# Routing of the first batch inside the state-space layer's last sequence, batches of 6, 5 and 5, and a third gather buffer

## The chip, the cores and the metric

The kernel runs on one core of a Trainium2 chip. The metric is the device time of one execution in microseconds (us); lower is better. Before the change the median of three runs is 1745.33 us (1744.99 to 1748.70).

The core's engines run side by side, each with its own instruction stream: PE multiplies matrices (weights are loaded by PEld), DVE does vector work, ACT applies functions, POOL does vector work too and issues the indirect DMAs (gathers and scatters), and SP issues the plain DMAs. They wait for each other by semaphores.

## The reference

The input is 16 sequences of 512 rows of 128 numbers. Four blocks follow each other, each with a residual and a layer norm:

```python
x = layernorm(x + linear_attention(x, W))                  # block 1
x = layernorm(x + moe32(x))                                # block 2: 32 experts, top 4, plus a shared expert
x = layernorm(x + mamba(x))                                # block 3: selective state space, 16 states
x = layernorm(x + moe8(x))                                 # block 4: 8 experts, top 2, plus a shared expert

def moe8(x):                       # xf: 8192 rows
    scores = softmax(xf @ gate_w.T)
    _, idx = top_k(scores + gate_b, 2)                     # the choice is by the biased scores,
    w = take_along_axis(scores, idx)                       # the weight by the unbiased ones
    expert(x) = silu((x @ w1 + b1) * (x @ w3 + b3)) @ w2 + b2
    return sum_k w[k] * expert[idx[k]](x) + shared_expert(x)

def mamba(x):                      # per sequence, d_inner 256
    xi, z = split(x @ in_proj.T); xc = silu(conv(xi))
    h_t = exp(dt_t * A) * h_(t-1) + dt_t * x_t * B_t       # 16 states, 512 steps
    y_t = sum_n h_t[n] * C_t[n] + D * x_t
    return (y * silu(z)) @ out_proj.T
```

## The kernel before

**Blocks 1 and 2** (0 to 376 us). The rows are normalized and stored with their gates in `xg_rows`. The 32 experts are worked through in eight groups of four. For a group, POOL gathers the rows (`xe<-xg_rows`, L759, four indirect DMAs), PE transposes and multiplies (L1255 to L1271), ACT and DVE form the gated product, DVE writes `ye` (L1651), and POOL adds the result into `resid_rows` (L767, four indirect DMAs). There are two `xe` buffers: the first two groups are gathered up front, and while group s is scattered, one scatter and one gather in turn, group s + 2 is gathered.

**Block 3** (376 to 1371 us). The 16 sequences run through a software pipeline, `schedule(iteration)`: in the turn of a sequence s, DVE scans its 16 states n one after the other (two scans `hst` of 512 steps, L1757, and for 12 of the 16 states the product `prod` with C, L1779; POOL makes the other four, L834); ACT makes the decays (L1029), POOL `dbx` (L825), PE sums over the states (L1340). In the same turn the front of the next sequence f (projections, convolution) and the end of the one before, m (`y` L1692, out-projection L1353, statistics L1511, scale and shift on POOL from L809, `x3o` on ACT), are spread over the states. In the last sequence's turn there is no f. Its place is used for the first batch of block 4: PE transposes its kept rows (L1363), ACT copies them (L1060), and PE scores them (L1372), one sequence at each of the states 7 to 12.

**Block 4** (1371 to 1741 us). The rows are cut into batches of 6, 6 and 4 sequences (`BATCH`). Of each batch DVE works out the routing: `scores` (row maximum and difference, L1705 and L1707), ACT the exponential (`soften`, L1070), `choose` and `choose_second` (L1713 to L1743, the two best of eight experts), PE counts (L1464), `place_rows` (L1847 to L1865) and `place_rows_end` (L1873 to L1892: the row numbers `row_of`, the gates and the table of units). Then POOL scatters the batch's rows, sorted by expert, into `sorted_rows` (`send_rows`, L880, two indirect DMAs a tile of 128 rows). PE runs 60 steps g: `N_FIRST` = 12 shared steps (one sequence each through the shared expert), then 44 routed units of 512 sorted rows (16, 16 and 12 in the three batches), then the other four shared steps (`LATE`). A step is L1421 (transpose), L1430, L1433, L1446 and L1456/L1457 on PE. The units' results are stored in `expert_rows`; POOL fetches them back (`fetch_rows`, L892, eight indirect DMAs a sequence) and DVE adds them up (`combine`) at the steps of `COMBINE_AT`. Rows of a batch can be fetched when all units of the batch are stored.

All orders are written out by hand: each engine's program lists its instructions in the order of the states and steps.

## Time and profile before

| | |
|---|---|
| median of three runs | 1745.33 us |
| profiled execution, its own time | 1742.75 us |
| its span | 1741.0 us |
| mean granted PE clock | 0.896 |
| PE busy | 1393.9 us, 80% |
| DVE busy | 1352.9 us, 78% |
| POOL busy | 1367.5 us, 79% |
| ACT busy | 972.2 us, 56% |
| POOL dbx L825, 256 of them | 613.8 us |
| DVE scans L1757, 512 of them | 592.0 us |
| POOL fetches L892, 128 of them | 124.5 us, 50.7 idle before them |
| POOL scatters L880, 128 of them | 125.9 us, 48.4 idle before them |

The profile is of one execution; its times stand beside its own 1742.75, which is 2.6 us below the median. The busy shares are means over four blocks that are limited by different engines: a share of 80% says nothing of what a stretch waits for. For that one reads a stretch at a time. An entry in square brackets names how long the engine was idle before an instruction and what ended the wait. "issue" is time in which the profile shows nothing that the engine waited for.

### The profile page before, as it was taken

The numbers are of one execution on the slowest core, as the hardware profiler recorded it, in microseconds if no ns is written. First come the engines' busy times: TensorE is split into PE (matmuls) and PEld (weight loads), VectorE is DVE, ScalarE is ACT, GpSimd is POOL, SyncE is SP. The second block draws the span as 40 slices with busy tenths as digits, with TensorE's granted clock in tenths as the row PEclk, the third lists the DMA queues.
The fourth block names the chain that finished last, engine by engine and source line by source line (L and its number), as shares of the span: only waits on it lengthen the run. The fifth ranks groups of instructions, "written<-read, shape, count | busy, mean of one in ns | idle before, by whom it ended". The sixth has DMA issues, their size and how long they took to land.

```text
span 1741.0 us, 23137 instructions
## 1 busy us (share of the span) xinstructions
PE 1393.9 (80%) x5849; PEld 832.6 (48%) x5890; DVE 1352.9 (78%) x2623; ACT 972.2 (56%) x1681; POOL 1367.5 (79%) x949
## 2 busy tenths in 40 slices
PE   5778744426998899889988998898897797999990
PEld 3666643312443344334433443343343476998970
DVE  3888831112999999999999999999999858657777
ACT  2665511104655665566556646655664465887873
POOL 2656566753999999999989989999999477777575
PEclk8999955557999999999989999999899999999995
DMA  5433243325382422342234123312521323555544
GB/s 149 127 101 121 84 89 59 43 40 187 117 254 115 141 84 73 123 140 73 80 127 140 62 86 132 133 56 90 178 80 55 118 69 97 165 155 155 147 107 135
DMA packets 195131, 195.44 MB, mean 112 GB/s; under 512 B 22520, under 2 KB 174008, under 8 KB 190776
## 3 DMA queue, kind: packets, MB, share of 16 engines
q1 hardware_dynamic: 172280, 168.95, 30.0%
q0 software_dynamic: 22784, 25.71, 7.3%
q8 instruction: 28, 0.46, 0.1%
q14 instruction: 39, 0.32, 0.1%
HBM read 137.26 MB, written 59.80 MB: 113 GB/s over the span
## 4 chain that ended last, share of the span: by engine, by line
PE 42%; DVE 26%; issue 15%; POOL 9%; ACT 2%; DMA 2%; DVEq 1%; SPq 1%; POOLq 0%; another core or an unknown queue 0%; ACTq 0%
PE bank L1340 13%; DVE hst L1757 12%; PE bank L1295 6%; PE bank L1433 2%; DVE prod L1779 2%; PE bank L1446 2%; POOL dbx L825 2%; PE bank L1430 2%; PE bank L1457 2%; PE bank L1456 2%; POOL yg L892 2%; PE bank L1329 1%; PE bank L1353 1%; PE bank L1293 1%; POOL xe L759 1%
## 5 line engine op out<-in xcount | busy, mean ns | idle before, releaser
L825 POOL TENSOR_TENSOR dbx<-u,ball 128x1024 f32<-128x1024 f32 x256 | 613.8, 2497 | 5.3 <-POOL u L862 2.8
L1757 DVE TENSOR_TENSOR_SCAN hst<-bank,dbx 128x512 f32<-128x512 f32 x512 | 592.0, 1205 | 11.2 <-POOL dbx L825 6.7
L1340 PE MATMUL bank<-prod,ident 128*128 128x512 f32 x1024 | 514.0, 639 | 23.4 <-DVE prod L1779 18.0
L1029 ACT ACTIVATE bank<-dt,aneg 128x511 f32<-128x511 f32 x512 | 346.4, 688 | 278.8 <-DVE hst L1757 276.8
L1340 PEld LDWEIGHTS bank<-prod,ident 128*128 128x128 f32 x1024 | 207.4, 205 | 263.6 <-issue 209.9
L1779 DVE TENSOR_TENSOR prod<-hst,bank 128x1024 f32<-128x1024 f32 x192 | 233.4, 1216 | 17.2 <-DVE hst L1757 13.8
L834 POOL TENSOR_TENSOR prod<-hst,call 128x1024 f32<-128x1024 f32 x64 | 161.0, 2515 | 22.9 <-DVE hst L1757 22.8
L892 POOL DMA_INDIRECT yg<-expert_rows,row_of x128 | 124.5, 972 | 50.7 <-issue 38.5
L1324 PE MATMUL bank<-parts,sel_c 128*128 128x512 bf16 x152 | 61.1, 403 | 73.8 <-DVE prod L1779 73.1
L1295 PE MATMUL bank<-x2T,inc 128*128 128x512 f32 x256 | 116.5, 598 | 0.0
L880 POOL DMA_INDIRECT sorted_rows<-x3b,row_of x80 | 79.3, 991 | 27.9 <-issue 25.3
L1324 PEld LDWEIGHTS bank<-parts,sel_c 128*128 128x128 bf16 x192 | 18.8, 98 | 132.5 <-DVE prod L1779 88.3
L1802 DVE SCALAR_TENSOR_TENSOR hg<-bank,wv,ha 128x256 f32<-128x256 f32 x88 | 38.5, 479 | 55.4 <-ACT ha L1083 55.1
L1295 PEld LDWEIGHTS bank<-x2T,inc 128*128 128x128 f32 x256 | 49.3, 193 | 62.7 <-issue 62.7
L694 POOL TENSOR_TENSOR dga<-rka,iota_a 128x2048 bf16<-128x2048 f32 x16 | 58.7, 3670 | 12.3 <-DVE ohb L1540 12.3
L1456 PE MATMUL bank<-wv,hg 128*128 128x128 f32 x352 | 68.1, 275 | 0.4 <-DVE acc L1833 0.4
L1457 PE MATMUL bank<-wv,hgb 128*128 128x128 f32 x352 | 68.2, 276 | 0.0
L767 POOL DMA_INDIRECT resid_rows<-ye,ixs x32 | 50.7, 1585 | 16.2 <-issue 13.7
L880 POOL DMA_INDIRECT sorted_rows<-x3a,row_of x48 | 46.6, 970 | 20.5 <-issue 13.4
L857 POOL TENSOR_TENSOR dt<-dtr,dta 128x1024 f32<-128x1024 f32 x16 | 40.7, 2545 | 27.3 <-ACT dta L1022 27.3
L1456 PEld LDWEIGHTS bank<-wv,hg 128*128 128x128 f32 x352 | 56.8, 192 | 3.2 <-DVE acc L1833 0.6
L710 POOL TENSOR_SCALAR rstd<-mv 128x4 f32<-128x4 f32 x16 | 3.6, 228 | 67.8 <-DVE mv L1584 67.8
(294 smaller groups left out, 2765.4 us busy)
## 6 DMA issues: line engine op xcount, KB each, us to landing
ball<-b_rows SPq DMA_DIRECT2D x32, 2048.0 KB, 7.1
call<-b_rows SPq DMA_DIRECT2D x16, 1024.0 KB, 9.5
xr<-sorted_rows SPq DMA_DIRECT2D x44, 256.0 KB
expert_rows<-yu SPq DMA_DIRECT2D x44, 256.0 KB, 2.7
sorted_rows<-blank SPq DMA_DIRECT2D x2, 4096.0 KB
xg_rows<-xg SPq DMA_DIRECT2D x16, 320.0 KB, 2.5
xt<-in_x SPq DMA_DIRECT2D x16, 256.0 KB, 2.9
xT<-in_xT SPq DMA_DIRECT2D x16, 256.0 KB, 3.1
```

Source lines behind the costliest of these rows:

```text
L825: gp.tensor_tensor(dbx[n % NDB][:, :, :], u[s.par][:, :, :], ball[:, n:n + 1, :].to_broadcast([P, NH, SEQ]), ALU.mult).then_inc(dbx_rdy, 1)
L834: gp.tensor_tensor(prod[2][:, :, :], hst[2][:, :, :], call[:, k:k + 1, :].to_broadcast([P, NH, SEQ]), ALU.mult).then_inc(pprod_rdy, 1)
L880: gp.indirect_dma_start(xs_d[b][:, :], bass.IndirectOffsetOnAxis(row_of[:, c, k:k + 1], 0), x3_tile(k), None).then_inc(sent[k % 2], 16)
L892: gp.indirect_dma_start(yg[q % 3][:, k, c, :], None, y_d[b][:, :], bass.IndirectOffsetOnAxis(row_of[:, c, q * TT + k:q * TT + k + 1], 0)). ...
L1029: act.activation(da_ps[h][:, 1:SEQ], dt_[s.par][:, h, 1:SEQ], ACT.Exp, scale=aneg[:, h, n:n + 1]).then_inc(da_rdy, 1)
L1295: last = mm(pb_ps[:, :], inc[:, k, tile(h)], x2T[:, k:k + SEQ], start=False, stop=(k == DCONV - 1))
L1324: mm(cb_ps[k % 2][:, :], sel_c[:, n, :], parts[s.par][:, :], start=True, stop=True).then_inc(cb_rdy, 1)
L1340: last = mm(y_ps[:, h, :], ident[:, :], from_[:, h, :], start=False, stop=(n == NS - 1), skip_group_check=True)
L1456: mm(yu_ps[g % 2][:, tile(k)], hg[g % 2][:, tile(k)], w[:, W2A:W2B], start=True, stop=False)
L1457: last = mm(yu_ps[g % 2][:, tile(k)], hgb[g % 2][:, tile(k)], w[:, W2B:BIAS], start=False, stop=True)
L1757: dve.tensor_tensor_scan(h_of[:, h, :], da_ps[h][:, :], dbx[n % NDB][:, h, :], 0.0, ALU.mult, ALU.add).then_inc(scan_rdy, 1)
L1779: tt(prod[k % 2][:, :, :], h_of[:, :, :], over_h(cb_ps[k % 2]), ALU.mult).then_inc(prod_rdy, 1)
```

## The change

1. **Third `xe` buffer.** `NXE = 3`: POOL gathers three groups up front, and group s + 3 while group s is scattered. The loops over groups on PE, DVE and POOL are written out. One wait on `xe_got` is added before the indices of the next gather.
2. **Routing of the first batch** moves on DVE from behind the last sequence into its turn: `scores` behind state 9's product, `choose` and `choose_second` in state 10, `place_rows` and `place_rows_end` behind state 11's product. The gates and the table of units are split off (`gates_and_units`) and stay behind y. ACT copies the kept rows at the states 3, 4, 6 (two), 7 (two), in place of one at each of 7 to 12, and its exponential `soften` stands in state 10.
3. **Scatters of the first batch**: five tiles (ten DMAs) on POOL at state 15, four tiles (eight) before the last scale and shift, the other thirty where all 48 stood.
4. **Batches of 6, 5, 5**, units 16, 14, 14. The shared step of sequence 1 goes from the first ones behind the units (`LATE` has five), and `COMBINE_AT` moves with it.

```diff
-BATCH = (6, 6, 4)
+BATCH = (6, 5, 5)
+NXE = 3
-LATE = (2, 3, 4, 5)
-S_ORDER = (0,) + tuple(range(6, NB)) + (1,) + LATE
+LATE = (1, 2, 3, 4, 5)
+S_ORDER = (0,) + tuple(range(6, NB)) + LATE
+KEPT_TURN = {3: ((0, None),), 4: ((1, None),), 6: ((2, 0), (3, 1)), 7: ((4, 2), (5, 3)), 8: ((None, 4), (None, 5))}
+SCORE_0, CHOOSE_0, COUNT_0, PLACE_0 = 9, 10, 11, 11
+SENT_FIRST, SENT_NEXT = 5, 4
-COMBINE_AT = [35, 37, 39, 41, 43, 45, 49, 51, 53, 56, 58, 60, 61, LAST, LAST, LAST]
+COMBINE_AT = [34, 36, 39, 41, 43, 45, 48, 50, 52, 55, 57, 61, 62, LAST, LAST, LAST]
-            xe = [eb(f"xe{p}", [P, EG, XGW]) for p in range(2)]
+            xe = [eb(f"xe{p}", [P, EG, XGW]) for p in range(NXE)]
...
# POOL, a group of experts
                 if ahead:
+                    gp.wait_ge(xe_got[ahead.par], ahead.half(16 * EG))
                     take_indices(ixg, ahead, ixg_rdy)
...
-            with gp.bass.Fori(0, E0 // EG // 2 - 1, engines=(gp.engine,), hint_back_edge=True) as j:
-                for i in (0, 1):
-                    group(Seq(j, i), Seq(j, i + 2))
-            group(Seq(0, E0 // EG - 2), None)
-            group(Seq(0, E0 // EG - 1), None)
+            for i in range(E0 // EG):
+                group(Seq(0, i), Seq(0, i + NXE) if i + NXE < E0 // EG else None)
...
# POOL, the state-space layer
             def iteration(f, s, m, ahead):
                 for n in range(NS):
+                    if s and not f and n == NS - 1:
+                        gp.wait_ge(ld_x3[0], X3_LOADS[0])
+                        send_rows(0, range(SENT_FIRST))
...
+                    if m and not s and n == 3:
+                        send_rows(0, range(SENT_FIRST, SENT_FIRST + SENT_NEXT))
                     if m and n == 4:
                         scale_shift(rs2, nm2, mv2, m, m_mv, m_rs, x3_rdy)
...
# DVE, the state-space layer
-                    if m and not s and n == 0:
-                        dve.wait_ge(pprod_rdy, NP * NB)
-                        scores(0)
                     if m and n == 0:
                         gated(m)
-                    if m and not s and n == 1:
-                        choose(0)
-                        choose_second(0)
+                    if m and not s and n == 0:
+                        gates_and_units(0)
...
+                    if s and not f and n == SCORE_0:
+                        dve.wait_ge(dt_rdy, NB)
+                        dve.wait_ge(u_rdy, NB)
+                        scores(0)
+                    if s and not f and n == CHOOSE_0:
+                        choose(0)
+                        choose_second(0)
+                    if s and not f and n == PLACE_0:
+                        place_rows(0)
+                        place_rows_end(0)
```

The batch's PE count goes to state 11, the two banks of `l1_ps` change places, and the tiles of block 4 in SBUF are laid out in another order.

DVE, from the last states of the last sequence on, before (`hst` are the scans of states, `l1m`, `l1s` the scores, `y2` the gated output, `l1z` the first instruction of `choose`):

```order
L1757 SCALAR_TENSOR_TENSOR hst1<-bank2,dbx3 128x512
L1757 SCALAR_TENSOR_TENSOR hst1<-bank3,dbx3 128x512
L1779 TENSOR_TENSOR prod1<-hst1,bank56 128x1024
L1705 TENSOR_REDUCE l1m<-lg0 128x24
L1707 TENSOR_TENSOR l1s<-lg0,l1m 128x192
L1692 TENSOR_TENSOR y2<-zs1,bank01 128x1024
L1713 TENSOR_REDUCE l1z<-l1e 128x24
L1715 RECIPROCAL l1r<-l1z 128x24
L1717 TENSOR_TENSOR sc1<-l1e,l1r 128x192
```

and now, at states 9 to 10 of the same sequence (lines have other numbers: L1833 is the scan, L1851 the product, L1719 and L1721 the scores, L1727 on `choose`):

```order
L1851 TENSOR_TENSOR prod0<-hst0,bank4 128x1024
L1719 TENSOR_REDUCE l1m<-lg0 128x24
L1721 TENSOR_TENSOR l1s<-lg0,l1m 128x192
L1833 SCALAR_TENSOR_TENSOR hst2<-bank2,dbx2 128x512
L1833 SCALAR_TENSOR_TENSOR hst2<-bank3,dbx2 128x512
L1727 TENSOR_REDUCE l1z<-l1e 128x24
L1729 RECIPROCAL l1r<-l1z 128x24
L1731 TENSOR_TENSOR sc1<-l1e,l1r 128x192
L1733 TENSOR_TENSOR bi1<-sc1,w_gb1 128x192
```

Scores and choice have moved from behind the last product to between the scans, with six more scan pairs behind them.

POOL, behind the last `dbx` of the last sequence, before (`hgb` are the memsets, `rs2` and `nm2` scale and shift):

```order
L825 TENSOR_TENSOR dbx3<-u1,ball 128x1024
L842 MEMSET hgb0 64x512
L843 MEMSET hgb0 64x512
L842 MEMSET hgb1 64x512
L843 MEMSET hgb1 64x512
L809 TENSOR_SCALAR rs2<-mv2 128x4
L811 TENSOR_TENSOR rs2<-rs2,neghalf 128x4
L814 TENSOR_TENSOR nm2<-mv2,rs2 128x4
L817 TENSOR_SCALAR nm2<-nm2 128x4
L880 DMA sorted_rows0<-x3a,row_of 8192x128 x48
```

and now (L849 is the send):

```order
L831 TENSOR_TENSOR dbx3<-u1,ball 128x1024
L849 DMA sorted_rows0<-x3a,row_of 8192x128 x10
L860 MEMSET hgb0 64x512
L861 MEMSET hgb0 64x512
L860 MEMSET hgb1 64x512
L861 MEMSET hgb1 64x512
L849 DMA sorted_rows0<-x3a,row_of 8192x128 x8
L815 TENSOR_SCALAR rs2<-mv2 128x4
L817 TENSOR_TENSOR rs2<-rs2,neghalf 128x4
L820 TENSOR_TENSOR nm2<-mv2,rs2 128x4
L823 TENSOR_SCALAR nm2<-nm2 128x4
L849 DMA sorted_rows0<-x3a,row_of 8192x128 x30
```

Ten sends now stand before the memsets and eight between these and the scale and shift.

ACT, in the last sequence, now (L1074 copies kept rows, L1041 makes decays):

```order
L1041 ACTIVATE bank2<-dt1,aneg 128x511
L1041 ACTIVATE bank3<-dt1,aneg 128x511
L1074 ACTIVATE xu0<-bank56 128x512
L1074 ACTIVATE xu1<-bank56 128x512
L1041 ACTIVATE bank2<-dt1,aneg 128x511
L1041 ACTIVATE bank3<-dt1,aneg 128x511
L1074 ACTIVATE xu0<-bank56 128x512
L1074 ACTIVATE xu1<-bank56 128x512
```

Before, each of the six copies stood alone between two pairs of decays; now four of them stand two by two.

## Rows read from the trace of the kernel before

**Rows 1.** the stretches view: us of the stretch, busy us and count by engine, granted clock
```profile
1311.00:1369.00 58.00, 48.20 (x172) 25.32 (x175) 54.84 (x58) 25.44 (x42) 45.92 (x27) 0.97 0.02 7
1396.90:1419.70 22.80, 22.80 (x139) 17.06 (x137) 8.82 (x13) 12.92 (x21) 17.27 (x19) 1.00 0.16 53
1484.60:1532.70 48.10, 48.10 (x323) 45.03 (x321) 28.47 (x61) 40.03 (x81) 35.59 (x36) 1.00 0.57 162
```

**Rows 2.** timeline of POOL, first expert layer: start, us, instruction, [idle before <-releaser]
```profile
270.81 0.18 POOL L756 COPY ixs<-idx 128x4 uint32 x1 [7.01 <-DVE ye L1651]
...
339.96 0.20 POOL L756 COPY ixs<-idx 128x4 uint32 x1
...
353.77 0.20 POOL L756 COPY ixs<-idx 128x4 uint32<-128x4 uint32 x1
...
366.05 0.19 POOL L756 COPY ixs<-idx 128x4 uint32<-128x4 uint32 x1 [3.45 <-DVE ye L1651]
```

**Rows 3.** timeline of DVE: y of three sequences, then the last sequence's end
```profile
487.20 1.22 DVE L1692 TENSOR_TENSOR y<-zs,bank 128x1024 f32<-128x1024 f32 x1 [0.35 <-PE bank L1340]
...
778.93 1.22 DVE L1692 TENSOR_TENSOR y<-zs,bank 128x1024 f32<-128x1024 f32 x1
...
1256.77 1.22 DVE L1692 TENSOR_TENSOR y<-zs,bank 128x1024 f32<-128x1024 f32 x1 [1.63 <-PE bank L1340]
...
1348.13 2.34 DVE L1757 TENSOR_TENSOR_SCAN hst<-bank,dbx 128x512 f32<-128x512 f32 x2 [1.11 <-ACT bank L1029]
...
1365.66 0.34 DVE L1705 TENSOR_REDUCE l1m<-lg 128x24 f32<-128x192 f32 x1
...
1367.82 1.22 DVE L1692 TENSOR_TENSOR y<-zs,bank 128x1024 f32<-128x1024 f32 x1 [1.42 <-PE bank L1340]
...
1375.40 0.83 DVE L1511 BATCH_NORM_STATS2 st<-bank 128x6 f32<-128x128 f32 x4
...
1376.68 0.33 DVE L1847 COPY tin<-bank 128x192 f32<-128x192 f32 x1
...
1381.62 0.19 DVE L1880 CAST row_of<-posf 128x48 uint32<-128x48 f32 x1
```

**Rows 4.** the chain of waits, last batch's fetches: start, us, what
```profile
1687.65 0.35 POOL yg L892
...
1726.52 0.94 POOL yg L892
```

**Rows 5.** timeline of DVE, end of the first expert layer
```profile
365.18 0.69 DVE L1651 TENSOR_TENSOR ye<-bank,ge 128x512 f32<-128x512 f32 x1 [4.20 <-PE bank L1271]
376.39 0.23 DVE L1783 TENSOR_SCALAR negb<-ident 128x128 bf16<-128x128 f32 x1 [10.52 <-DMA resid_rows<-ye,ixs]
```

**Rows 6.** timeline of ACT, last sequence: a copy of kept rows
```profile
1346.82 0.60 ACT L1060 ACTIVATE xu<-bank 128x512 f32<-128x512 f32 x1 [2.58 <-PE bank L1363]
```

**Rows 7.** timeline of PE: out-projection, first new sequence, first unit
```profile
1369.09 2.05 PE L1353 MATMUL bank<-w_outp,y 128*128 128x128 f32 x16 [0.46 <-DVE y L1692]
...
1380.13 1.09 PE L1421 MATMUL bank<-ident,x3b 128*128 128x128 f32 x4 [3.95 <-DMA x3b<-x_rows]
...
1450.50 0.63 PE L1421 MATMUL bank<-ident,xr 128*128 128x128 f32 x4 [0.25 <-DMA xr<-sorted_rows]
1454.85 0.89 PE L1421 MATMUL bank<-ident,xr 128*128 128x128 f32 x4 [3.72 <-ACT xu L1065]
```

**Rows 8.** timeline of POOL behind the last scan
```profile
1364.55 0.52 POOL L842 MEMSET hgb<- 64x512 f32 x1 [7.09 <-DVE hst L1757]
...
1376.95 0.23 POOL L809 TENSOR_SCALAR rs<-mv 128x4 f32<-128x4 f32 x1 [10.20 <-DVE mv L1515]
```

**Rows 9.** the page's groups: POOL's long product
```profile
L825 POOL TENSOR_TENSOR dbx<-u,ball 128x1024 f32<-128x1024 f32 x256 | 613.8, 2497 | 5.3 <-POOL u L862 2.8
```

**Rows 10.** one line each: durations ns min/median/max, first and last start
```profile
L1579 DVE TENSOR_TENSOR gm<-lexp,mask x16: 272/273/336, 41.2 to 227.1; 128x128 f32<-128x128 f32 x16
...
L811 POOL TENSOR_TENSOR rs<-rs,neghalf x32: 1036/1040/1165, 386.7 to 1377.3; 128x4 f32<-128x4 f32 x32
```

More of the change, by code:

```diff
@@ L367, in build @@
         tab = sb("tab", [P, 2 * N_UNIT], I32)
+        ha = [sb(f"ha{k}", [P, SEQ]) for k in range(2)]
+        hab = [sb(f"hab{k}", [P, SEQ]) for k in range(2)]
+        hg = [sb(f"hg{k}", [P, SEQ]) for k in range(2)]
+        hgb = [sb(f"hgb{k}", [P, SEQ]) for k in range(2)]
+        yu = [sb(f"yu{k}", [P, TT, D]) for k in range(3)]
+        yg = [sb(f"yg{k}", [P, TT, 2, D]) for k in range(3)]
+        st3 = sb("st3", [P, TT, 6])
+        mv3 = sb("mv3", [P, NB * TT, 2])
+        rs3 = sb("rs3", [P, NB * TT])
+        nm3 = sb("nm3", [P, NB * TT])
         wall = sb("wall", [P, E1, WCOLS])
@@ L783, in group @@
                         gather(ahead, k)
-            for i in (0, 1):
+            for i in range(NXE):
+                need(gp, xe_got[i % 2], 16 * EG * (i // 2))
                 take_indices(ixg, Seq(0, i), ixg_rdy)
@@ L1039, in iteration @@
                         front(f, n)
-                    if s and not f and 7 <= n < 7 + KEPT:
-                        kept_up(n - 7)
-                    if s and not f and n == 7 + KEPT:
+                    if s and not f and n in KEPT_TURN:
+                        for k, scored in KEPT_TURN[n]:
+                            if k is not None:
+                                kept_up(k)
+                    if s and not f and n == SCORE_0 - 1:
                         act.wait_ge(l1_mm, KEPT)
@@ L1254, in group @@
                 for k in range(EG):
-                    last = pe.transpose(bank[2][:, tile(k)], xe[s.par][:, k, 0:D], ident[:, :])
+                    last = pe.transpose(bank[2][:, tile(k)], xe[s.off % NXE][:, k, 0:D], ident[:, :])
                 last.then_inc(xeT_mm, 1)
@@ L1272, in group @@
                 last.then_inc(dn_mm, 1)
-            with pe.bass.Fori(0, E0 // EG // 2, engines=(pe.engine,), hint_back_edge=True) as j:
-                for i in (0, 1):
-                    group(Seq(j, i))
+            for i in range(E0 // EG):
+                group(Seq(0, i))
             def front(s, n):
@@ L1396, in iteration @@
                         out_proj(m)
-                    if s and not f and 7 < n <= 7 + KEPT:
-                        kept_score(n - 8)
-                    if s and not f and 7 <= n < 7 + KEPT:
-                        kept_turn(n - 7)
+                    if s and not f and n in KEPT_TURN:
+                        for k, scored in KEPT_TURN[n]:
+                            if scored is not None:
+                                kept_score(scored)
+                            if k is not None:
+                                kept_turn(k)
+                    if s and not f and n == COUNT_0:
+                        count(0)
             pe.wait_ge(added, E0 // 2 * 16)
@@ L1664, in _ @@
             group(Seq(0, 1))
-            with dve.bass.Fori(1, E0 // EG // 2, engines=(dve.engine,), hint_back_edge=True) as j:
-                for i in (0, 1):
-                    group(Seq(j, i))
+            for i in range(2, E0 // EG):
+                group(Seq(0, i))
             def stats_ahead(s):
```

171 lines of the change are left out of this document (82 added, 89 removed).

## The prediction, made before the changed kernel was run

> **What bounds the kernel now.** I read the page's busy shares first: no engine is at its limit over the whole span, so the stages have to be read one by one. [rows 1] gives three stretches. In the last sequence of the state-space layer (1311 to 1369) DVE is busy 54.84 of 58.00 us and PE 48.20. In four shared steps of the last layer (from 1396.9) PE is busy throughout at full clock, 22.80 us for four, 5.70 each, and DVE needs 8.82, 2.2 a step. In ten routed units (from 1484.6) PE is again full, 48.10 us, 4.81 each, and DVE has 28.47, 2.8 a unit. Then the timelines, engine by engine, where the edit moves work. In the first expert layer POOL's indirect DMAs set the pace [rows 2]. In the last sequence DVE's chain of scans does [rows 3]. At the very end POOL does once more: fetch after fetch, the chain of waits being nothing but POOL L892 and its issue gaps [rows 4].
>
> **A. Third gather buffer, first expert layer: -8.4 us.** In [rows 2] a group of four scatters with four gathers takes 339.96 to 353.77, 13.8 us; one with scatters alone runs from 353.77 to 362.60 (366.05 less the 3.45 of idle time before it), 8.8 us. The four gathers are the difference, 5.0, 1.25 each. Before, two groups are without gathers; now three are, and the four gathers taken away stand up front, before the first scatter. Up front POOL idles 7.01 us before 270.81, waiting for DVE's first ye: the four gathers (5.0) and a copy of indices fit. So one group gets shorter by 13.8 - 8.8 = 5.0. The second gain: POOL waits 3.45 us before 366.05 for DVE's ye at 365.18 [rows 5]; the last group's rows now arrive a whole group earlier, so ye is done when POOL comes. Sum 5.0 + 3.4 = 8.4. The layer's end hangs on the last scatter: DVE waits 10.52 us for resid_rows at 376.39 [rows 5]. The new wait on `xe_got` names gathers issued a group ago: nothing. Loops written out cost or save nothing that a row shows. Bounds: 0 (something else sets the group's pace) and -9 (issue gaps go too).
>
> **B. Routing of batch 0 inside the last sequence: +16.5 us.** A state costs DVE 3.5 us there: from 1348.13 to 1365.66 are five of them, 17.5 us, with one wait, of 1.11 [rows 3]. So nothing that is put in is hidden. What is put in, with its durations from where it stood: scores two instructions behind 1365.66, 0.34 us the first, 0.74 together; choose, first and second best, from y's end at 1369.0 to the statistics at 1375.40, 6.4; place 1376.68 to 1381.81, 5.1; together 12.2 [rows 3]. On top come waits. The copies of kept rows come two to a turn now, and ACT's exponentials stand behind them: ACT waited 2.58 us for PE before a single such copy [rows 6], and DVE's scans take what the exponentials make; l1e is asked for one state after the scores, with an exponential pair in front of it on ACT; the count on PE answers after two small matmuls. I take 1 + 1 + 1 us for pairs of copies, 0.8 for the rest, and 0.5 for issue between small instructions: 12.2 + 3.8 + 0.5 = 16.5.
> What it takes away behind the sequence is less than it seems. Before, choose stood between y (1367.82) and the statistics (1375.40) and held these back 4.3 us, the end of PE's out-projection being 1371.1 [rows 7]. But PE's first shared step on a new sequence waits for the DMA x3b until 1380.13, 3.95 us [rows 7], and that load is issued when the out-projection is done, whatever DVE does. x3o, which PE's last matmul group of the first shared step waits for, is held from the other side: POOL's scale_shift began at 1376.95, 12.4 us after the last scan (1364.55) [rows 8]. Now four memsets (2.2) and eight sends stand before it on POOL, at the fetches' price of [rows 4] 8 x 1.25 = 10.0: 12.2 us. It stays where it was, relative to the scans. So the whole stretch moves by A + B = +8.1. The ten sends ahead of the memsets take 12.5 us, and the four states behind place 14.0: they fit.
> Bounds: +2 if the bursts met idle time of DVE (1.1 of wait and some of PE's slack), +21 with a low clock in PE's longer pauses and waits at their rows' sizes. I stay near the sum of rows, since the stretch has 3 us of idle time in 58.
>
> **C. Scatters begun early: 0.** 18 of 48 sends are gone before the first shared step. Before, the first unit got its rows just in time: PE waited 0.25 us at 1450.50 for xr. What held it was ACT, 3.72 us before 1454.85 [rows 7], with table loads for batch 1's softmax. With the rows earlier the ACT wait remains. The later batches have 40 sends each in place of 48 and 32, all beside work.
>
> **D. Order of the last layer: -3 us.** The shared step of sequence 1 goes behind the units (11 first, 5 late). The number of steps is the same, 16 and 44. Up to the last unit's end one shared step less: -5.7. Against that, the bursts of batch 1 and 2 (choose 6.4, place 5.1 and the gates at 24 tiles, somewhat less at the 20 that both have now) fall more on units, where DVE has 4.81 - 2.8 = 2.0 us free, than on shared steps, where it has 5.7 - 2.2 = 3.5 [rows 1]. Two steps on which DVE was hidden and now is not, some 1.35 us each: +2.7. Sum -3; bounds -12 (the ACT wait and all bursts vanish) and +1.
>
> **E. The tail: +10.0 us.** The last batch has five sequences. Its rows can be fetched only when its last unit is stored, and this unit is the last but for the late shared steps. Before, 32 fetches run one by one from 1687.65, when the store has landed, to 1727.46 (1726.52 + 0.94), 1.25 us each [rows 4]; now 40. 8 x 1.25 = 10.0, with DVE and ACT waiting for them. The late shared steps (one more, 5.7) are hidden beneath. Bounds: 8 and 11.
>
> **Sum.** -8.4 + 16.5 + 0 - 3 + 10.0 = +15.1 against the profiled execution of 1742.75 (span 1741.0): 1757.9. The median of the runs shown is 2.6 above it; the forecast against it is 1745.33 + 15.1 = 1760.4.
>
> **Rivals.**
> 1. *Contention between DVE and POOL in the inserted bursts, 1767.* DVE's long instructions in the sequences read one operand from PSUM; choose and place are the first with two operands from SBUF beside POOL's long products (2.50 us each [rows 9]). Two rows bear on it: `gm<-lexp,mask` takes 272 to 273 ns fifteen times and 336 once, `rs<-rs,neghalf` 1036 to 1040 and once 1165 [rows 10], and these are the two that overlap an instruction of that kind on the other engine. If each of the three or so products that POOL still owes in choose's stretch and one in place's holds DVE up, that is up to 4 x 2.50 = 10.0, less what stands beside single-operand work: some +6, or 1766.4. Against it: both lengthenings are small, 0.06 and 0.13 us. The Trainium skill, "SBUF — State Buffer", section "SBUF: two separate sides", says that a VectorE instruction with two SBUF inputs and a GpSimd instruction that reads SBUF exclude each other for their whole length. By that rule the price is that of this rival; the trace agrees in sign and doesn't show the size.
> 2. *The bursts are absorbed, 1746, not slower.* If the last sequence is held by something else than DVE (PE's accumulation, ACT's exponentials), B is its lower bound, +2, and the sum is -8.4 + 2 - 3 + 10.0 = +0.6. It decides at the point where DVE has about 12 us of waits between 1311 and 1366. For it: PE also is busy 48 of 58. Against it: [rows 3] shows the scans back to back.
> 3. *The sequences change pace, 1749.* The y's of the first five intervals are 58.35 us apart (487.20 to 778.93), of the next eight 59.73 (778.93 to 1256.77) [rows 3]. Nothing in the program differs between them. If another start or other places in memory gave all the short pace, 8 x 1.38 = 11.0 would come off: 1749.4. It can as well go the other way.
> 4. *The buffer gains nothing, 1769.* A = 0: PE's and DVE's chain of one group would have to be as long as POOL's 13.8; DVE is busy far less.
> 5. *The clock.* PE's granted clock is 0.97 in the last sequence [rows 1], against 1.00 later. 0.97 over 58 us is 3.5 us at the lower of its two levels (1.2 in place of 2.4 GHz), a loss of some 1.7. If PE's pauses beside the two bursts double or treble that, it is +2 to +4, 1763. The Trainium skill, "TensorE: Matmul & The Clock Gate", Part 1, has the array fall to half its clock when little work reached it; by that rule both bursts end in slow matmuls, but those hide beneath scans unless PE is what DVE waits for. It is inside the forecast's range.
>
> **Chances.** Forecast as summed, 1755 to 1764: 0.47. Rival 1: 0.25. Rival 2: 0.08. Rival 3 (shorter pace): 0.12. Rival 4: 0.08. The range 1749 to 1771 leaves out most of rival 2 and the far ends of 1 and 4. About 0.2%, 3.5 us, is what a measurement of this kernel can tell from no change. Faster than that has 0.04 (rival 2 with D at its lower bound), within it 0.09 (rival 2 and a little of 3), slower 0.87.
>
> **What the changed profile would show.** A: the last group of scatters ends 8 us earlier than 374.6, with no wait of POOL for ye before it. B: y of the last sequence about 8 us later than 1367.8; the interval to the y before it 71 us instead of 54; DVE at 3.5 us a state but for three gaps. Rival 1 would show small DVE instructions of 0.36 us taking 2 to 3. C: the wait of ACT's table loads at the first unit still there. E: 40 fetches after the last unit's store, 51 us. I am wrong if the last sequence grows by less than 12 us, or if the time between the last unit's store and the end grows by less than 8.

## The result, and the profile after

| | before | changed |
|---|---|---|
| median | 1745.99 us (4 runs) | 1761.62 us (4 runs) |
| profiled execution, its span | 1742.75, 1741.0 | 1761.27, 1759.6 |
| mean granted PE clock | 0.896 | 0.887 |

The ratio is 1.009, 95% interval 1.0072 to 1.0108: 15.6 us slower by the medians, forecast 15.1. Between the two profiled executions lie 18.6 us. The traces put them at these places, each read as the distance of two instructions, before and after:

| stretch | forecast | measured |
|---|---|---|
| up to the first expert group's indices (252.55, 251.46) | 0 | -1.1 |
| A: from there to DVE's first instruction behind the layer (123.84, 114.46) | -8.4 | -9.4 |
| from there to y of the last sequence but one (936.99, 939.08) | 0 | +2.1 |
| B: from that y to the last sequence's y (54.44, 77.89) | +16.5 | +23.4 |
| C, D: from y to the first L1430 behind the last unit's own (310.72, 304.92) | -3 | -5.8 |
| E: from there to the start of the last fetch (49.22, 59.33) | +10.0 | +10.1 |
| the rest (13.24, 12.46) | 0 | -0.8 |

"To the last unit" means in what follows to the mark of the row C, D, with which PE starts the step behind the last unit (L1454 in the changed kernel).

**A.** POOL's timeline in the first expert layer: start, us, engine, line, instruction, idle before and its end.

```profile
269.30 0.18 POOL L763 COPY ixs<-idx 128x4 uint32<-128x4 uint32 x1 [1.41 <-DVE ye L1666]
...
338.20 0.19 POOL L763 COPY ixs<-idx 128x4 uint32<-128x4 uint32 x1
...
346.38 0.77 POOL L763 COPY ixs<-idx 128x4 uint32<-128x4 uint32 x1
...
354.97 0.78 POOL L763 COPY ixs<-idx 128x4 uint32<-128x4 uint32 x1
```

and DVE's first instruction behind it:

```profile
365.92 0.23 DVE L1865 TENSOR_SCALAR negb<-ident 128x128 bf16<-128x128 f32 x1 [16.06 <-DMA resid_rows<-ye,ixs]
```

These answer to [rows 2, 5]. POOL's idle time before the first scatter went from 7.01 to 1.41 us; there are three groups without gathers now (338.20 to 346.38, to 354.97, and the last), 8.2 to 8.6 us each; the wait of 3.45 us for ye is gone. From the first group's indices to the last scatters' landing the layer is 9.4 us shorter.

**B.** The last sequence as a whole (stretch, then busy us of PE, PEld, DVE, ACT, POOL, the granted clock), against the first of [rows 1]:

```profile
1305.00:1383.00 78.00, 51.96 (x170) 26.50 (x171) 67.26 (x85) 24.99 (x41) 53.91 (x37) 0.82 0.04 12
```

DVE's timeline in it (L1833 is the scan, L1719 to L1757 the scores and choose, L1768 to L1801 place, L1706 y):

```profile
1305.00 1.19 DVE L1706 TENSOR_TENSOR y<-zs,bank 128x1024 f32<-128x1024 f32 x1
...
1334.26 2.34 DVE L1833 TENSOR_TENSOR_SCAN hst<-bank,dbx 128x512 f32<-128x512 f32 x2 [5.06 <-ACT bank L1041]
...
1338.82 2.58 DVE L1833 TENSOR_TENSOR_SCAN hst<-bank,dbx 128x512 f32<-128x512 f32 x2 [0.97 <-ACT bank L1041]
...
1342.57 0.35 DVE L1719 TENSOR_REDUCE l1m<-lg 128x24 f32<-128x192 f32 x1
...
1346.60 0.35 DVE L1727 TENSOR_REDUCE l1z<-l1e 128x24 f32<-128x192 f32 x1 [1.04 <-ACT l1e L1084]
...
1347.32 0.88 DVE L1731 TENSOR_TENSOR sc<-l1e,l1r 128x192 f32<-128x192 f32 x1
1348.23 2.38 DVE L1733 TENSOR_TENSOR bi<-sc,w_gb 128x192 f32<-128x192 f32 x1
1350.64 0.35 DVE L1740 TENSOR_REDUCE bm<-bi 128x24 f32<-128x192 f32 x1
1351.03 1.99 DVE L1742 TENSOR_TENSOR eq<-bi,bm 128x192 f32<-128x192 f32 x1
1353.06 0.36 DVE L1744 TENSOR_TENSOR eq<-eq,rev_e 128x192 f32<-128x192 f32 x1
...
1361.23 1.35 DVE L1770 TENSOR_TENSOR_SCAN run<-restart,tin 128x192 f32<-128x192 f32 x1
...
1366.60 0.19 DVE L1801 CAST row_of<-posf 128x48 uint32<-128x48 f32 x1
...
1382.89 1.22 DVE L1706 TENSOR_TENSOR y<-zs,bank 128x1024 f32<-128x1024 f32 x1 [2.08 <-PE bank L1353]
```

The y's of the last two sequences are 77.89 us apart. Three things are to be seen. First, four waits: 5.06 and 0.97 us for ACT's decays, 1.04 for l1e, 2.08 for PE before y, 9.15 together, where [rows 3] have 1.11 and 1.42: +6.6, for which the forecast had 3.8. Second, the instructions of choose have not all their old length: `sc` takes 0.88 us, `bi` 2.38, the first `eq` 1.99 and `run` 1.35, where they took 0.36, 0.36, 0.36 and 0.56 before: 5.0 us more. The row between them, a maximum over one operand, keeps its 0.35, and so does the next `eq`, at 1353.06. Third, the rest of the bursts, 12.2 us, is as forecast; but the scores, 0.7 of it, stood between these two y's before as well, so only 11.4 are new. 11.4 + 6.6 + 5.0 = 23.0; measured 23.4, and most of the other 0.4 stands in two pairs of scans that take 2.58 and 2.46 us in place of 2.33.

What POOL does meanwhile (L840 and L831 are its long products, L849 the sends):

```profile
1345.63 2.35 POOL L840 TENSOR_TENSOR prod<-hst,call 128x1024 f32<-128x1024 f32 x1 [5.85 <-DVE hst L1833]
1347.94 4.87 POOL L831 TENSOR_TENSOR dbx<-u,ball 128x1024 f32<-128x1024 f32 x2
1359.82 2.35 POOL L831 TENSOR_TENSOR dbx<-u,ball 128x1024 f32<-128x1024 f32 x1 [7.01 <-DVE hst L1833]
1367.64 1.13 POOL L849 DMA_INDIRECT sorted_rows<-x3a,row_of  x1 [5.48 <-DVE row_of L1801]
...
1380.18 0.54 POOL L860 MEMSET hgb<- 64x512 f32 x1
...
1392.63 0.23 POOL L815 TENSOR_SCALAR rs<-mv 128x4 f32<-128x4 f32 x1
```

Its products end at 1347.98, about 1350.4 and 1352.81, and at 1362.17. The four stretched instructions end at 1348.20, 1350.61, 1353.02 and 1362.58: each 0.2 to 0.4 us behind the end of a product that was running when it came. From 1352.81 until 1359.82 POOL has no product, and choose goes on at 0.36 us each.

ACT's timeline before the wait of 5.06 us (L1074 copies kept rows):

```profile
1331.61 0.60 ACT L1074 ACTIVATE xu<-bank 128x512 f32<-128x512 f32 x1 [5.19 <-PE bank L1376]
1332.95 0.60 ACT L1074 ACTIVATE xu<-bank 128x512 f32<-128x512 f32 x1 [0.75 <-PE bank L1376]
```

The first copy of a pair waited 5.19 us for PE, and the decays of state 6 stand behind both copies. PE's matmuls in front of that copy's transposes (L1353, the sums over the states), and the next four:

```profile
1323.68 6.61 PE L1353 MATMUL bank<-prod,ident 128*128 128x512 f32 x8 [3.27 <-POOL prod L840]
...
1332.97 1.88 PE L1353 MATMUL bank<-prod,ident 128*128 128x512 f32 x4
```

The eight took 0.83 us each, the four 0.47: the granted clock is 0.50 from 1322.8 to 1329.6, the lower level. So two things are in this wait, the pair of copies and PE's clock; e6 and e12 take them apart.

**C and D.** PE's timeline behind the last sequence and at the first units (L1445 transposes, L1457 and L1480 are the later products of a step):

```profile
1384.16 2.05 PE L1366 MATMUL bank<-w_outp,y 128*128 128x128 f32 x16 [0.46 <-DVE y L1706]
...
1393.07 1.08 PE L1445 MATMUL bank<-ident,x3b 128*128 128x128 f32 x4 [6.42 <-DMA x3b<-x_rows]
...
1461.12 0.66 PE L1445 MATMUL bank<-ident,xr 128*128 128x128 f32 x4 [0.69 <-ACT xu L1079]
...
1472.48 0.49 PE L1480 MATMUL bank<-wv,hg 128*128 128x128 f32 x2 [3.29 <-DVE acc L1915]
...
1490.49 2.07 PE L1457 MATMUL bank<-xu,wv 128*128 128x256 f32 x4 [3.22 <-DVE hg L1884]
```

The first row's end, 1386.2, is 15.1 us later than before [rows 7]; the sequence's load x3b comes only 12.9 us later (1393.07 against 1380.13): the wait is for all loads of a batch, and the batch has five sequences in place of six. The first unit waits 0.69 us for ACT, not 3.72: the two table loads of 1.28 us each stand in front of that copy no more (1449.97 and 1451.60 before), but behind the first unit's (1466.18 and 1467.82). The routing of batch 1 now stands in PE's way twice, 3.29 and 3.22 us.

**E.** POOL's first fetch of the last batch, and the end of the chain of waits (start, us, what):

```profile
1697.28 0.94 POOL L904 DMA_INDIRECT yg<-expert_rows,row_of  x1 [16.69 <-DMA expert_rows<-yu]
```

```profile
1747.14 3.47 DMA yg<-expert_rows,row_of
```

40 fetches take 50.8 us, 1.27 each, the last starting at 1747.14. POOL had been idle for 16.69 us before them; in [rows 4] it came straight from the fetches of the batch in front. With 6, 6 and 4 sequences the 48 fetches of the middle batch end just when the last unit is stored, with 6, 5 and 5 they are done long before, and the batch that nothing hides is larger.

### The profile page after: what moved, and what is told of

Read it like the earlier page. It is cut to its first block, busy times and chain, and to the rows that moved or that the text cites. A ratio compares the mean times of both kernels' runs of the same rounds, so it can differ in the third digit from the quotient of the medians.

```text
span 1759.6 us, 22955 instructions
## 1 busy us (share of the span) xinstructions
PE 1409.1 (80%) x5850; PEld 838.9 (48%) x5890; DVE 1358.3 (77%) x2623; ACT 972.5 (55%) x1681; POOL 1368.1 (78%) x949
## 4 chain that ended last, share of the span: by engine, by line
PE 43%; DVE 27%; issue 16%; POOL 8%; ACT 2%; DMA 1%; DVEq 1%; SPq 1%; POOLq 0%; another core or an unknown queue 0%; ACTq 0%
PE bank L1353 13%; DVE hst L1833 13%; PE bank L1308 6%; DVE prod L1851 2%; PE bank L1457 2%; PE bank L1470 2%; PE bank L1454 2%; PE bank L1480 2%; POOL yg L904 2%; PE bank L1481 2%; PE bank L1306 2%; PE bank L1366 2%; PE bank L1342 1%; POOL resid_rows L774 1%; PE bank L1320 1%
## 5 line engine op out<-in xcount | busy, mean ns | idle before, releaser
L831 POOL TENSOR_TENSOR dbx<-u,ball 128x1024 f32<-128x1024 f32 x256 | 614.3, 2502 | 11.8 <-DVE hst L1833 7.0
L1833 DVE TENSOR_TENSOR_SCAN hst<-bank,dbx 128x512 f32<-128x512 f32 x512 | 592.0, 1204 | 13.3 <-ACT bank L1041 8.9
L1353 PE MATMUL bank<-prod,ident 128*128 128x512 f32 x1024 | 524.6, 650 | 21.5 <-DVE prod L1851 16.8
L1041 ACT ACTIVATE bank<-dt,aneg 128x511 f32<-128x511 f32 x512 | 346.6, 688 | 302.4 <-DVE hst L1833 299.3
L1353 PEld LDWEIGHTS bank<-prod,ident 128*128 128x128 f32 x1024 | 210.9, 208 | 267.1 <-issue 215.7
L1851 DVE TENSOR_TENSOR prod<-hst,bank 128x1024 f32<-128x1024 f32 x192 | 233.4, 1216 | 19.1 <-DVE hst L1833 13.8
L840 POOL TENSOR_TENSOR prod<-hst,call 128x1024 f32<-128x1024 f32 x64 | 161.4, 2522 | 34.9 <-DVE hst L1833 34.8
L849 POOL DMA_INDIRECT sorted_rows<-x3b,row_of x80 | 79.5, 994 | 41.2 <-issue 26.1
L1480 PE MATMUL bank<-wv,hg 128*128 128x128 f32 x352 | 68.8, 278 | 3.3 <-DVE acc L1915 3.3
L849 POOL DMA_INDIRECT sorted_rows<-x3a,row_of x48 | 46.3, 964 | 23.2 <-issue 12.6
L1480 PEld LDWEIGHTS bank<-wv,hg 128*128 128x128 f32 x352 | 57.3, 194 | 6.3 <-DVE acc L1915 3.7
L701 POOL TENSOR_TENSOR dgb<-rkb,iota_b 128x1024 bf16<-128x1024 f32 x16 | 34.7, 2171 | 26.8 <-DVE rkb L1621 26.8
```

Source lines behind the costliest of these rows:

```text
L701: gp.tensor_tensor(dst[:, :, :], a, b, ALU.subtract).then_inc(done, 1)
L831: gp.tensor_tensor(dbx[n % NDB][:, :, :], u[s.par][:, :, :], ball[:, n:n + 1, :].to_broadcast([P, NH, SEQ]), ALU.mult).then_inc(dbx_rdy, 1)
L840: gp.tensor_tensor(prod[2][:, :, :], hst[2][:, :, :], call[:, k:k + 1, :].to_broadcast([P, NH, SEQ]), ALU.mult).then_inc(pprod_rdy, 1)
L849: gp.indirect_dma_start(xs_d[b][:, :], bass.IndirectOffsetOnAxis(row_of[:, c, k:k + 1], 0), x3_tile(k), None).then_inc(sent[k % 2], 16)
L1041: act.activation(da_ps[h][:, 1:SEQ], dt_[s.par][:, h, 1:SEQ], ACT.Exp, scale=aneg[:, h, n:n + 1]).then_inc(da_rdy, 1)
L1353: last = mm(y_ps[:, h, :], ident[:, :], from_[:, h, :], start=False, stop=(n == NS - 1), skip_group_check=True)
```

## The experiments

Each was run beside the kernel before on the same chip; "faster" and "slower" are against that.

| run | median us | before us | ratio, 95% interval |
|---|---|---|---|
| e1, three gather buffers alone | 1739.30 | 1748.51 | 0.9945 (0.9931 to 0.9959) |
| e2, batches 6, 5, 5 alone | 1758.91 | 1748.51 | 1.0068 (1.0050 to 1.0086) |
| e3, routing in the last sequence and early sends alone | 1774.27 | 1748.51 | 1.0152 (1.0133 to 1.0171) |
| e4, four gather buffers alone | 1741.68 | 1748.51 | 0.9957 (0.9943 to 0.9972) |
| e5, changed kernel without early sends | 1763.40 | 1747.67 | 1.0093 (1.0071 to 1.0116) |
| e6, changed kernel, one copy a state | 1764.03 | 1747.67 | 1.0099 (1.0074 to 1.0123) |
| e7, e5 with the bursts at the last states | 1754.64 | 1747.67 | 1.0030 (1.0017 to 1.0044) |
| e8, before with DVE products, SBUF and PSUM | 1741.58 (one) | 1750.77 (one) | |
| e9, before with DVE products, SBUF and SBUF | 1883.15 (one) | 1750.77 (one) | |
| e10, e8 again | 1744.79 | 1748.29 | 0.9980 (0.9968 to 0.9992) |
| e11, e1 and e8 together | 1738.13 | 1748.29 | 0.9941 (0.9925 to 0.9956) |
| e12, e6 without early sends | 1756.16 | 1748.29 | 1.0043 (1.0029 to 1.0057) |

### The parts one by one: e1, e2, e3

```diff
# e1, on the kernel before
+NXE = 3
...
-            xe = [eb(f"xe{p}", [P, EG, XGW]) for p in range(2)]
+            xe = [eb(f"xe{p}", [P, EG, XGW]) for p in range(NXE)]
# e2, on the kernel before
-BATCH = (6, 6, 4)
+BATCH = (6, 5, 5)
-LATE = (2, 3, 4, 5)
+LATE = (1, 2, 3, 4, 5)
# e3, on the changed kernel
-BATCH = (6, 5, 5)
+BATCH = (6, 6, 4)
-                    if ahead:
-                    gp.wait_ge(xe_got[ahead.par], ahead.half(16 * EG))
```

Expected of e1: 

> The kernel before with part A alone: three gather buffers and the group loops written out. Theory (terms add up): the last scatter of the first expert layer ends 8 to 10.5 us earlier, as in the changed kernel (365.9 instead of 376.4 for DVE's first instruction behind it), and the whole kernel gains 8 to 10 us, some 1736 to 1738 against the before of the same rounds. Rival (phase of the sequences): in the changed kernel the long intervals between the y's (59.7 instead of 58.35) begin one and a half sequences earlier and give 2.7 of the gain back; if that belongs to the earlier start, it is seen here too (12 us gained at the third y, 9.5 at the thirteenth). Rival (the buffer gains nothing): 1746.

Measured: 9.2 us by the medians. In its trace the expert layer takes 114.47 us between the marks of A, as in the changed kernel. The long intervals begin after three short ones, as in the changed kernel, and give 2.2 us of it back up to the fourteenth y.

Expected of e2: 

> The kernel before with batches of 6, 5, 5 alone (five late shared steps, the combining steps moved with it); routing and buffers as before. Theory: D -3 to -4 and E +10, sum +6 to +7: 40 fetches behind the last unit's store in place of 32, and POOL idle some 15 us before them, since it has only 40 to do beside 14 units. If D is nothing: +10. If the tail is hidden by something: 0 or below.

Measured: +10.4, more than expected. Last unit to last fetch is 59.3 us (+10.1, E). But D came out at +1.8 instead of -3 to -4. PE's timeline says why:

```profile
1381.11 1.09 PE L1421 MATMUL bank<-ident,x3b 128*128 128x128 f32 x4 [1.73 <-DMA x3b<-x_rows]
...
1454.28 1.09 PE L1421 MATMUL bank<-ident,xr 128*128 128x128 f32 x4 [7.45 <-DMA xr<-sorted_rows]
```

With one shared step less the first unit comes 5.7 us earlier, and its rows are not there: 7.45 us for the DMA xr. The load x3b, awaited for five sequences and not six, gives 2.2 back.

Expected of e3: 

> The changed kernel with batches of 6, 6, 4 and with two gather buffers: of the change, the routing inside the last sequence and the early sends remain (B and C). Theory from the changed kernel's trace: the last sequence takes 77 to 78 us in place of 54.4 (+23.5), of which 2 come back at the load x3b and up to 3 at the last unit's rows; the total is +18 to +22. By the prediction's own term it would be +16.5. If the early scatters paid, it would be under +12.

Measured: +25.8. The last sequence takes 76.56 us (+22.1), and the wait for x3b is the longest of all:

```profile
1409.99 1.09 PE L1447 MATMUL bank<-ident,x3b 128*128 128x128 f32 x4 [8.54 <-DMA x3b<-x_rows]
```

From y to the last unit it needs 313.1 us, 2.3 more than before: with 12 shared steps in front the first unit doesn't wait for rows, so rows that come early are worth nothing. It waits for ACT, 4.16 us, as C had it.

So the parts do not add up: -9.2 + 10.4 + 25.8 = +27.0, and the whole is +15.6. Of the 11.4 between, 9.9 are found in one stretch, from y to the last unit: +1.8 in e2, +2.3 in e3, -5.8 in both together. Routing early and one shared step less need each other: the first makes the rows be there, the second makes use of them.

### More buffers: e4

```diff
# on e1
-NXE = 3
+NXE = 4
```

Expected: 

> As e1, with four gather buffers: the gathers of four groups stand up front. In the changed kernel POOL has 1.4 us of idle time left before its first scatter, so four more gathers (5.0) push this back by 3.6, and one group more is without gathers (-5.0 to -5.6): -1.4 to -2 against e1. Rival: POOL's sum of indirect DMAs is the bound and PE's chain of a group comes next (9.3 us, groups without gathers take 8.2 to 8.8 already): nothing or a loss of 1 to 4.

Measured: 115.45 us for the layer, 1.0 more than with three. The rival's size was right: the front is full, the first scatter starts 3.8 us later than in e1, and the groups give only 2.8 of it back. The fourth group from the end, now without gathers, takes 10.5 us and not 8.2 to 8.6; 2.8 of it is idle time of POOL for which the trace names no cause ("issue"), so the rival's reason, PE's chain of a group, is not shown.

### The early sends: e5

```diff
# on the changed kernel, POOL
-                    if s and not f and n == NS - 1:
-                        gp.wait_ge(ld_x3[0], X3_LOADS[0])
-                        send_rows(0, range(SENT_FIRST))
-                    if m and not s and n == 3:
-                        send_rows(0, range(SENT_FIRST, SENT_FIRST + SENT_NEXT))
-            send_rows(0, range(SENT_FIRST + SENT_NEXT, KEPT * TT))
+            gp.wait_ge(ld_x3[0], X3_LOADS[0])
+            send_rows(0, range(KEPT * TT))
```

Expected: 

> The changed kernel with all 48 scatters of the first batch behind the last scale and shift, where they stood before; nothing sent early. Theory (C is worth nothing by itself): within 2 us of the changed kernel, 1760 to 1763: x3o comes 2 to 4 us earlier, the first unit's rows later. Rival (the early sends hide what the routing costs): 5 us or more slower than the changed kernel, with PE waiting for the DMA xr before the first unit.

Measured: 1.0093 against 1.009, no difference. Stretch by stretch there is one: from y to the last unit 306.9 us in place of 304.9, so the sends bring 2.0 us, and from the expert layer's end to the last y but one 935.3 in place of 939.1, since the long intervals begin two sequences later here. The total can't tell the first from the second. PE doesn't wait for rows at the first unit without the sends either: it is the early routing, not the early sending, that has them ready.

### Where the last sequence loses: e6, e12, e7

```diff
# e6, on the changed kernel; e12: the same on e5
-KEPT_TURN = {3: ((0, None),), 4: ((1, None),), 6: ((2, 0), (3, 1)), 7: ((4, 2), (5, 3)), 8: ((None, 4), (None, 5))}
-SCORE_0, CHOOSE_0, COUNT_0, PLACE_0 = 9, 10, 11, 11
+KEPT_TURN = {3: ((0, None),), 4: ((1, None),), 6: ((2, 0),), 7: ((3, 1),), 8: ((4, 2),), 9: ((5, 3),), 10: ((None, 4), (None, 5))}
+SCORE_0, CHOOSE_0, COUNT_0, PLACE_0 = 11, 12, 13, 13
# e7, on e5
-SCORE_0, CHOOSE_0, COUNT_0, PLACE_0 = 9, 10, 11, 11
+SCORE_0, CHOOSE_0, COUNT_0, PLACE_0 = 13, 14, 15, 15
```

Expected of e6: 

> The changed kernel with the copies of the kept rows one a state (3, 4, 6, 7, 8, 9) in place of two at states 6 and 7, and therefore with scores at state 11, choose at 12, place at 13. Theory: DVE's wait of 5.06 us for ACT's decays at the first pair of copies goes to about 1, and fewer of POOL's long products remain beside choose, so its stretched instructions (4.2 us over their 0.36 in all) shrink too: 4 to 8 us faster than the changed kernel. Rival (the wait is PE's low clock and not the pair): within 1 us.

Measured: the last sequence takes 70.48 us, 7.4 less than in the changed kernel, and the total doesn't fall. The stretched instructions shrink as expected, from 5.0 us over their own length to 0.8. The wait does not go to about 1:

```profile
1332.16 2.34 DVE L1833 TENSOR_TENSOR_SCAN hst<-bank,dbx 128x512 f32<-128x512 f32 x2 [3.67 <-ACT bank L1041]
```

PE's clock is at the lower level from 1321.9 to 1328.7 here too. The four waits of 9.15 us are 6.1 now. In the total, the gain turned into a new wait on PE:

```profile
1396.38 2.07 PE L1470 MATMUL bank<-xu,wsh 128*128 128x512 f32 x2 [6.84 <-ACT x3o L1068]
```

POOL's 18 sends come later relative to the scans, the scale and shift stand behind them, and PE's first shared step waits 6.84 us for x3o.

Expected of e12: 

> e6 (one copy of kept rows a state) without the early sends. In e6 the last sequence was 7.4 us shorter than in the changed kernel, but PE then waited 6.84 us for x3o, since POOL had 18 sends in front of the scale and shift. Theory: without them this wait is gone, and the total is 6 to 9 us under e5 and the changed kernel: about 1754 to 1757, like e7. Rival: something else eats it: 1762 to 1764.

Measured: 1.0043, 7.2 us better than e5 by the medians. The wait for x3o is gone, and that part of the theory holds. But the last sequence takes 72.90 us, 2.4 more than in e6, a gain and a larger loss. The wait for the decays is down to 0.82 us, at the same order of instructions up to there as in e6; the granted clock is 1.00 there (1323.5 to 1331.7), and PE's eight matmuls take 3.70 us in place of 6.61:

```profile
1326.66 3.70 PE L1349 MATMUL bank<-prod,ident 128*128 128x512 f32 x8 [3.28 <-POOL prod L840]
```

```profile
1332.99 2.34 DVE L1829 TENSOR_TENSOR_SCAN hst<-bank,dbx 128x512 f32<-128x512 f32 x2 [0.82 <-ACT bank L1037]
```

So with one copy a state the clock makes 2.9 us of that wait; at the lower level the pair makes 1.4 more (5.06 against 3.67). Then one instruction of the scores, with two SBUF operands, takes 5.92 us instead of 0.36, beside three products of POOL that follow each other without a pause:

```profile
1346.31 5.92 DVE L1717 TENSOR_TENSOR l1s<-lg,l1m 128x192 f32<-128x192 f32 x1
```

```profile
1345.04 6.97 POOL L831 TENSOR_TENSOR dbx<-u,ball 128x1024 f32<-128x1024 f32 x3
```

It ends at 1352.23, the third product at 1352.01. In the changed kernel `bi` got in between two such products, at 1350.4; why `l1s` did not stays open.

Expected of e7: 

> As e5 (no early sends), with scores at state 13, choose at 14 and place behind state 15's product, where POOL has hardly any long product left. Theory (VectorE instructions with two SBUF operands wait for POOL's long products): choose's sc, bi and eq take 0.36 us each again, as in the kernel before, where POOL was idle, and run takes 0.56; 4 to 5 us less than e5 from that alone. Rival (those instructions are slow for another reason of that place, such as the layout of their tiles): they keep 0.9, 2.4, 2.0 and 1.35 us.

Measured: 1.0030, 8.8 us better than e5 by the medians; the last sequence takes 69.69 us in place of 77.80. Its sc, bi, eq and run on DVE:

```profile
1360.84 0.36 DVE L1727 TENSOR_TENSOR sc<-l1e,l1r 128x192 f32<-128x192 f32 x1
1361.23 0.36 DVE L1729 TENSOR_TENSOR bi<-sc,w_gb 128x192 f32<-128x192 f32 x1
...
1362.01 0.36 DVE L1738 TENSOR_TENSOR eq<-bi,bm 128x192 f32<-128x192 f32 x1
...
1370.58 0.56 DVE L1766 TENSOR_TENSOR_SCAN run<-restart,tin 128x192 f32<-128x192 f32 x1
```

and POOL's last products and its first memset:

```profile
1347.94 6.99 POOL L831 TENSOR_TENSOR dbx<-u,ball 128x1024 f32<-128x1024 f32 x3
1369.08 0.52 POOL L857 MEMSET hgb<- 64x512 f32 x1 [14.15 <-DVE hst L1829]
```

The products end at 1354.9, before the bursts, and the four instructions have 0.36 and 0.56 us again. In e5, where choose stands beside the products, they have 0.88, 2.37 and 1.99, and run has 1.36. These four are 5.0 us of the 8.1 by which the last sequence is shorter; the other 3.1 are waits, for l1e and before y, that are gone.

### The suspected cost by itself: e8, e9

```diff
# on the kernel before, DVE, in front of prod; e9 has h_of[:, 1, at:at + 96] in place of cb_ps
                         need(dve, y_mm, s.at(ND, k - 1))
+                        if f and n in (5, 8):
+                            for at in (0, 96, 192):
+                                tt(xu[0][:, at:at + 96], h_of[:, 0, at:at + 96], cb_ps[k % 2][:, at:at + 96], ALU.mult)
```

Expected of e8: 

> The kernel before with six more DVE products of 128x96 in each of the first 15 sequences (three at state 5, three at state 8, into a tile that nothing reads): one operand from SBUF, one from PSUM. 90 instructions of about 0.25 us: +15 to +25 us by either theory, each instruction at its own length.

Expected of e9: 

> As e8, but both operands from SBUF. Theory (such an instruction and a long product of POOL exclude each other): many of the 90 instructions are stretched by the rest of a product of 2.3 us; at least 2 a sequence by 1.2 on average, +36 us over e8, at most all by 2.3, +210. Rival: the same time as e8 within 5 us.

Measured: the added products, ns min/median/max, of e8 and then of e9:

```profile
L1781 DVE TENSOR_TENSOR xu<-hst,bank x90: 246/249/256, 447.5 to 1282.6; 128x96 f32<-128x96 f32 x90
```

```profile
L1781 DVE TENSOR_TENSOR xu<-hst x90: 257/2392/2412, 448.5 to 1419.4; 128x96 f32<-128x96 f32 x90
```

The same 90 instructions of the same shape: 0.25 us with one operand in PSUM, 1.79 us on average (median 2.39, the length of a product of POOL) with both in SBUF, and e9 takes 142 us longer than e8, in one execution of each; 90 x (1.79 - 0.25) = 139. Each of the 75 stretched ones ends 0.1 us behind the end of a product of POOL, and the products keep their 2.36 us in the median. The exclusion is shown.

e8 itself was not as expected: no +15 to +25 but less time than the kernel before, 9.2 us less in a single execution; the five rounds of e10 leave 3.5.

### More work, less time: e10, e11

e10 is e8 in five rounds; e11 has the diffs of e1 and e8.

Expected of e10: 

> The kernel of e8 again, timed in five rounds. In its one profile the sequences were 58.8 us apart where they are 59.35 and 60.13 in the kernel before, DVE's waits for PE before y were 1.7 us instead of 12.0, and the granted clock 0.96 instead of 0.94, in spite of 17.5 us more work on DVE. Theory (the place of PE's pauses sets how often its clock falls, and more work on DVE moved them): 2 to 6 us faster than the kernel before. Rival (one lucky run): the same as before or up to 4 slower.

Expected of e11: 

> Three gather buffers (e1) and the six idle DVE products of e8 together. Theory: both gains add up, -9.4 for the buffer and -2 to -6 for the pace, and the 2 us that e1 lost by beginning the long intervals earlier come back: 11 to 16 us under the kernel before, faster than e1. Rival: as e1, -9.

Measured: e10 is 0.2% faster, interval 0.1 to 0.3%; e11 is as fast as e1, the two gains did not add up. The stretch from the first y to the fourteenth, before and in e8 (busy us of PE, PEld, DVE, ACT, POOL, then the clock):

```profile
487.00:1257.00 770.00, 688.05 (x1738) 308.05 (x1769) 730.15 (x846) 475.28 (x742) 727.23 (x405) 0.94 0.34 114
```

```profile
487.80:1253.60 765.80, 673.75 (x1737) 303.17 (x1769) 741.32 (x924) 475.90 (x741) 726.24 (x404) 0.96 0.34 114
```

DVE's waits there, before and then in e8:

```profile
DVE y L1692 <- PE bank L1340: 12.0, 10, 1.8
DVE xc L1681 <- ACT tc L991: 5.2, 13, 0.7
```

```profile
DVE y L1692 <- PE bank L1340: 1.7, 4, 1.0
```

DVE has 11 us more work, and from y to y the stretch is 3.8 us shorter (765.8 against 769.6). PE's 1738 matmuls take 688 us before and 674 in e8, at a granted clock of 0.94 and 0.96; DVE's waits for PE before y fall from 12.0 to 1.7 us. The y's are 58.8 us apart in e8 but for one interval of 59.8, in place of 59.35 and 60.13 by turns. The profile of e10, the same kernel, has three long intervals, 60.1, 59.8 and 59.8, and is only 1.4 us shorter than before over this stretch; its clock is 0.96 too. That PE was slower at the lower clock, and that y waited for it, is shown. That the moved pauses of PE keep the clock up is only argued, and what makes the long intervals begin after two, three or five short ones (none in e4, two in e2 and e3, three in e1, e6 and e12, five in e5, e7 and the kernel before) stays open. e11's intervals go to 60.8 by turns: the phase is not under control.

The Trainium skill, "TensorE: Matmul & The Clock Gate", Part 1, makes the clock follow how busy the array has been; the rows agree in direction, 0.82 in the changed kernel's last sequence with its long pauses against 0.97 before.

## Why the prediction held, point by point

**Direction and total: right, the total by luck.** The mechanism, bursts of DVE's routing between scans that had no idle time to hide them, is what the trace shows; e7 and e12 remove waits and stretched instructions around the bursts and get part of the time back. That the sum came within 0.5 us is luck: B was 6.9 us too small, errors of the other sign in A, D and beside the terms leave 3.4 between the profiled executions, and the medians happen to lie 2.9 closer. The last sequence was to take 71 us and took 77.9, and the sign that the prediction gave for rival 1, instructions of 0.36 us that take 2 to 3, is there: 2.38 and 1.99.

**A, -8.4: -9.4.** The step was right in both halves. The microsecond on top came from the front, where the first scatter starts 0.4 us earlier, and from groups without gathers of 8.2 to 8.6 us and not 8.8.

**B, +16.5: +23.4. This is the step that failed, by size.** One term was too small and one was missing. The waits (3.8) were 6.6: the row of [rows 6], 2.58 us before one copy, was taken at 1 us a pair, and it was 5.19. Rival 5, the clock, is in that: a granted clock of 0.82 over 78 us is some 28 us at PE's lower level, against 3 before (0.97 over 54), and by e6 and e12 some 2.9 us of the wait of 5.06 come from it, inside the rival's +2 to +4. And instructions that last longer than their rows had no term; they made 5.0. Rival 1 had named them, priced them at +6 and given them 0.25. Against these, the 0.5 for issue was not needed, and the scores' 0.7 us were counted as new though they stood in the same interval before. The two rows of [rows 10] that spoke for it were read as small; they were small because the overlap in each was only 0.2 to 0.3 us. The Trainium skill, "SBUF — State Buffer", section "SBUF: two separate sides", states the exclusion; e8 and e9 agree with it, 250 ns against 1785 on average, and it should have had the greater weight.

**C, 0: right within what the total can tell** (e5); by stretches the sends bring 2.0 us. Its reason, that the wait of 3.72 us for ACT's table loads remains, holds with 12 shared steps in front (4.16 in e3) and not with 11 (0.69).

**D, -3: -5.8 with C**, -3.8 without the early sends (306.9 in e5 against 310.7). The loads of a batch of five, 2.2 us earlier, were not seen. That the routing's early rows are what lets a shared step be left out in front was not seen either; taken alone (e2), D is +1.8.

**E, +10.0: +10.1.** Right in size and mechanism. One reading was off: the prediction took 1687.65 to 1727.46 for the last batch's 32 fetches, but that begins inside the last fetch of the batch in front. The batch's own first starts at 1688.35 and its last at 1727.76, 1.26 us each all the same.

**Beside the terms.** The sequences' pace gave back 2.1 us, rival 3 with the other sign. The errors of the table, -1.1, -1.0, -2.8 and -0.8 against +6.9, +2.1 and +0.1, leave 3.4 between the profiled executions and 0.5 between the medians; the total was forecast better than its parts. Rivals 2 and 4 are out: the bursts were not absorbed, and the buffer alone gains 0.55%.

**The better version** is e1 (or e11, which can't be told from it): three gather buffers alone, 0.9945 of the kernel before.

## What to carry to other kernels

When the engine that sets a stretch has no idle time, what is moved into the stretch costs its own length, the waits of everything queued behind it, and whatever it contends for: look at what kinds of operands the neighbours use before taking a duration from a quiet place. Put instructions with two SBUF operands on VectorE where GpSimd runs no long product, or give one operand a place in PSUM. A wait for another engine can be that engine's clock: look at the granted clock of the stretch before blaming the order of instructions (3.67 against 0.82 us here). Cut batches so that the work behind the last one is smallest, and see whether the engine that serves it was idle before (16.69 us here) or busy to the last moment.
